# Three stack fills moved from ScalarE to GpSimd memsets, one semaphore per stack, and new orders on all engines

## The reference

```python
# 1: a convolution layer: bias, separable FIR upsampling by 2, leaky ReLU, FIR downsampling by 2
out = sep_upfirdn(input + bias, up_filter * 2, up=2)
out = leaky_relu(out, 0.2) * sqrt(2)
x = sep_upfirdn(out, down_filter, down=2)
# 2: attention on the 256 points of each image, 8 heads of 16 channels
x_norm = group_norm(x, g1, b1, 32 groups)
q, k, v = split(qkv_w @ x_norm + qkv_b)
attn = softmax(q k^T / sqrt(16)); a = out_w @ (attn v) + out_b
# 3: a gated MLP with 512 hidden channels, and a residual
a = group_norm(a, g2, b2, 32 groups)
h1, gate = split(mlp1_w @ a); return x + mlp2_w @ (silu(h1) * gate)
```

## Time and profile before

| | us |
|---|---|
| three executions | 145.64, 146.48, 148.33 (median 146.48) |
| the profiled execution | 146.12 |
| its span, first to last instruction | 144.3 |
| TensorE busy in it | 137.9 (96%) |
| ScalarE busy | 101.9 (71%) |
| VectorE busy | 94.0 (65%) |
| GpSimd busy | 69.4 (48%) |

### The profile page before, as it was taken

The page is one execution under the profiler, slowest core; times in us unless marked ns, Lnnn a source line. Parts: engine busy times, 40 slices in busy tenths (PEclk is TensorE's granted clock), DMA queues, the critical chain, the costliest instruction groups (busy, mean ns, idle before and its releaser), DMA issues.

```text
span 144.3 us, 3301 instructions
## 1 busy us (share of the span) xinstructions
PE 137.9 (96%) x1150; PEld 121.2 (84%) x1150; DVE 94.0 (65%) x194; ACT 101.9 (71%) x233; POOL 69.4 (48%) x121
## 2 busy tenths in 40 slices
PE   6999899999979999999999999999999999999992
PEld 5797789999969687779699699797897997999991
DVE  6959343477547878698799999573784714743251
ACT  6957878654639689398685996697886995966330
POOL 8300560840770595300870304894305898689930
PEclk9999999999999999999999999999999999999999
DMA  3899204564620160611604305210010010011012
GB/s 105 275 298 336 93 0 115 152 170 136 163 75 0 51 174 3 173 50 49 174 2 136 92 2 163 59 36 0 9 36 2 0 35 8 0 41 36 0 36 73
DMA packets 12368, 12.12 MB, mean 84 GB/s; under 512 B 1600, under 2 KB 11328, under 8 KB 12352
## 3 DMA queue, kind: packets, MB, share of 16 engines
q1 hardware_dynamic: 12208, 11.81, 27.6%
q10 hardware_dynamic: 144, 0.10, 0.2%
HBM read 4.50 MB, written 1.05 MB: 38 GB/s over the span
## 4 chain that ended last, share of the span: by engine, by line
PE 79%; SPq 8%; DMA 6%; DVE 4%; issue 1%; ACT 0%; POOL 0%; ACTq 0%; POOLq 0%
PE pm L852 11%; PE ps L878 11%; PE po L903 10%; SPq L287 5%; PE pf L765 4%; DMA win<-in_xh 4%; PE px L765 4%; PE pf L767 4%; PE pf L766 4%; PE pf L780 3%; PE px L766 3%; PE px L767 3%; SPq L314 3%; PE po L926 3%; PE ps L780 2%; PE px L834 2%
## 5 line engine op out<-in xcount | busy, mean ns | idle before, releaser
L1541 DVE TENSOR_REDUCE neg_max<-pm 128x2 f32<-128x512 f32 x64 | 42.0, 683 | 12.5 <-PE pm L852 12.2
L530 ACT ACTIVATE up_t<-ps 128x512 f32<-128x512 f32 x64 | 35.8, 596 | 7.3 <-PE ps L878 4.1
L878 PE MATMUL ps<-q_stack,k_stack 128*128 128x256 f32 x128 | 27.9, 301 | 0.9 <-DMA q_stack<-max_row 0.9
L852 PE MATMUL pm<-k_stack,q_stack 127*128 127x256 f32 x128 | 27.9, 305 | 0.2
L421 POOL TENSOR_TENSOR gated_lo<-win,gated_hi 128x512 fp32r<-128x512 f32 x14 | 18.1, 1299 | 16.4 <-ACT gated_hi L585 16.4
L852 PEld LDWEIGHTS pm<-k_stack,q_stack 127*128 127x128 f32 x128 | 19.6, 189 | 3.4 <-issue 1.5
L878 PEld LDWEIGHTS ps<-q_stack,k_stack 128*128 128x128 f32 x128 | 19.7, 189 | 2.4 <-DMA q_stack<-max_row 1.1
L903 PE MATMUL po<-up_t,v_aug 128*32 128x256 f32 x256 | 15.7, 382 | 0.0
L765 PE MATMUL pf<-xm_hi,w_hi 128*128 128x256 f32 x44 | 13.3, 303 | 0.2 <-issue 0.2
L585 ACT ACTIVATE gated_hi<-win 128x512 fp32r<-128x512 f32 x14 | 8.8, 631 | 5.3 <-DVE win L1590 3.4
L766 PE MATMUL pf<-xm_lo,w_hi 128*128 128x256 f32 x44 | 12.3, 280 | 0.0
(11 more groups left out here) (150 smaller groups left out, 334.4 us busy)
## 6 DMA issues: line engine op xcount, KB each, us to landing
q_stack<-qk_parts SPq DMA_DIRECT2D x24, 128.0 KB, 2.4
k_stack<-qk_parts SPq DMA_DIRECT2D x24, 128.0 KB, 2.4
win<-in_xw SPq DMA_DIRECT2D x12, 128.0 KB, 3.2
win<-in_xh SPq DMA_DIRECT2D x6, 256.0 KB, 5.0
out<-win SPq DMA_DIRECT2D x8, 128.0 KB, 1.7
win<-in_w SPq DMA_DIRECT2D x1, 512.0 KB, 3.7
w_s<-in_w SPq DMA_DIRECT2D x1, 256.0 KB, 3.7
wqk_s<-in_wqk SPq DMA_DIRECT2D x1, 128.0 KB, 4.2
```

The costliest lines, as they stand in the source:

```text
L530: act.activation(probs[:, h // HALF, h % HALF, :, :].rearrange("p c n -> p (c n)"), ps[:, h % 2, :], ACT.Exp, scale=D ** -0.5).then_inc(pr ...
L852: return pe.matmul(pm[:, h % 2, c * N:(c + 1) * N], stack_rows(q_stack, i, slice(0, TOP))[:, h, c * 128:(c + 1) * 128], stack_rows(k_stack ...
L878: return pe.matmul(ps[:, h % 2, c * N:(c + 1) * N], stack_rows(k_stack, i, slice(0, TOP + 1))[:, h, c * 128:(c + 1) * 128], stack_rows(q_s ...
L1541: dve.tensor_reduce(neg_max[:, i % 2, 2 * h:2 * h + 2], pm[:, h % 2, :].rearrange("p (c n) -> p c n", c=2), AX.X, ALU.max, negate=True).th ...
```

## The change

ScalarE keeps one fill (the q stack of slot 1). The k stack of slot 1 and both stacks of slot 2 are set by memsets on GpSimd, at the head of its list. Each slot has its own semaphore `stack_clear[r]`, which `stack(i)` waits for. The lists of all five engines stand in a new order.

```diff
-        stacks_clear = sem("stacks_clear")
-        first_clear = sem("first_clear")
+        stack_clear = [sem(f"stack_clear{r}") for r in range(SLOTS)]
...
-                if i == 0:
-                    sp.wait_ge(first_clear, 2)
-                elif i < SLOTS:
-                    sp.wait_ge(stacks_clear, 2 * i)
+                if i < SLOTS:
+                    sp.wait_ge(stack_clear[i], 2)
...
+            def clear_stack(r, j):
+                pool.memset((q_stack, k_stack)[j][r][:, :, :].rearrange("p h n -> p (h n)").bitcast(F32), j * 1.0).then_inc(stack_clear[r], 1)
...
+            clear_stack(1, 1)
+            clear_stack(2, 0)
             constants()
             clear_values()
+            clear_stack(2, 1)
             split_wqk()
...
-            def fill(r, j):
-
-                act.activation((q_stack, k_stack)[j][r][:, :, :].rearrange("p h n -> p (h n)"),
-                               rest[:, j:j + 1].to_broadcast([128, HEADS * N]), ACT.Copy).then_inc(stacks_clear, 1)
+            def fill():
+
+                act.activation(q_stack[1][:, :, :].rearrange("p h n -> p (h n)"),
+                               rest[:, 0:1].to_broadcast([128, HEADS * N]), ACT.Copy).then_inc(stack_clear[1], 1)
...
-            dve.memset(rest[:, 0:1], 0.0).then_inc(rest_ready, 1)
-            dve.memset(rest[:, 1:2], 1.0).then_inc(rest_ready, 1)
+            dve.memset(rest[:, :], 0.0).then_inc(rest_ready, 1)
```

More of the change, by code:

```diff
@@ L325, in store @@
                 sp.dma_start(out[b], result[:, b * N:(b + 1) * N]).then_inc(stored, 16)
-            stack(0)
-            stack(1)
+            for j in range(0, 3):
+                stack(j)
             load_w1()
-            stack(2)
             rows(0)
@@ L607, in _ @@
             read_y(1)
-            leaky(5)
-            fill(2, 0)
-            for j in range(6, 10):
+            for j in range(5, 8):
                 leaky(j)
-            fill(2, 1)
-            high_parts(0)
             read_y(2)
             read_y(3)
+            leaky(8)
+            high_parts(0)
+            leaky(9)
             leaky(10)
@@ L620, in _ @@
             read_y(4)
-            for j in range(12, 15):
-                leaky(j)
+            leaky(12)
+            leaky(13)
             read_early_v(1)
+            leaky(14)
+            high_parts(2)
             leaky(15)
-            high_parts(2)
             read_y(5)
@@ L632, in _ @@
             exponentials(0, 1)
-            high_parts(3)
+            read_early_v(2)
+            sum_biases()
             exponentials(0, 2)
             exponentials(0, 3)
-            sum_biases()
+            high_parts(3)
             exponentials(0, 4)
+            exponentials(0, 5)
             read_rows(1)
-            for j in range(5, 8):
-                exponentials(0, j)
+            exponentials(0, 6)
+            exponentials(0, 7)
             read_early_v(3)
+            read_sums(0)
@@ L675, in _ @@
[L675 removed]
+            square_attn(2)
             squash(0)
[L677 to L679 removed]
             high_parts(7)
+            split_high(0)
+            read_sums(3)
             squash(1)
[L682 removed]
             exponentials(4, 0)
             exponentials(4, 1)
[L685 removed]
+            spread_inverse(3)
+            for j in range(2, 5):
+                exponentials(4, j)
+            read_proj(3)
@@ L716, in _ @@
-            spread_inverse(5)
-            for j in range(3, 6):
-                exponentials(6, j)
-            read_proj(5)
+            squash(3)
+            read_sums(5)
+            exponentials(6, 0)
+            exponentials(6, 1)
+            split_high(3)
+            exponentials(6, 2)
+            spread_inverse(5)
+            exponentials(6, 3)
+            squash(4)
+            exponentials(6, 4)
+            read_proj(5)
+            exponentials(6, 5)
+            square_attn(5)
@@ L1001, in _ @@
             downsample(1)
-            upsample(5)
-            upsample(6)
+            for j in range(5, 8):
+                upsample(j)
             group_means(0)
-            for j in range(7, 10):
-                upsample(j)
             downsample(2)
+            downsample(3)
+            upsample(8)
             project_qk(0)
-            downsample(3)
+            group_means(1)
+            upsample(9)
             upsample(10)
             project_v(0)
-            group_means(1)
             upsample(11)
@@ L1019, in _ @@
             maxima(0, 1, 1)
-            upsample(12)
+            upsample(13)
             maxima(0, 2, 0)
-            upsample(13)
             maxima(0, 2, 1)
+            project_v(1)
             maxima(0, 3, 0)
@@ L1028, in _ @@
             maxima(0, 4, 1)
-            project_v(1)
+            project_qk(2)
             maxima(0, 5, 0)
@@ L1368, in _ @@
             weigh(6, 1, 1)
+            turn_maxima(7)
             up_project(6, 0, 0)
+            down_project(4, 0)
+            down_project(4, 1)
             up_project(6, 0, 1)
+            up_project(6, 1, 0)
+            turn_sums(6)
+            up_project(6, 1, 1)
+            turn_inverse(6)
             scores(7, 0, 0)
```

561 lines of the change are left out of this document (271 added, 290 removed).

## The result

The changed kernel is slower: 150.08 us median of four executions (149.46 to 150.46), against 147.1 us for the kernel before on the same chip. The ratio is 1.0233 with a 95% interval of 1.0128 to 1.0337. So it is slower, clear of noise; whether by more than 2% stays open. The forecast was 145.4 us in a range of 143.0 to 147.4, and a result over 149.4 had been given a chance of 0.04: it missed on the side, not just the size. The profiled execution took 150.46 us with a span of 148.6.

The account below looks back on a forecast made before the run. TensorE, busy 137.9 of 144.3 us, was taken as the bound, so only its waits counted. Terms 0.8 - 0.5 + 0.4 = 0.7 us off the profiled 146.12 gave 145.4 us, range 143.0 to 147.4.

Parts of the forecast that it names:

- The fills: Start, ScalarE to GpSimd: three memsets end by about 10.5 us, long before use, so moving them costs 0.
- 12 to 20 us: TensorE's hole before the group means at 15.06 takes `upsample(7)`: gain 0.87 us, bounds 0 and 1.3.
- First swap of SyncE: `load_w1` behind `stack(2)`: first scores at 41.1 instead of 42.35; TensorE stays 0.8 us ahead, bounds -0.4 and 1.5.
- The sum so far: Start through the first scores: TensorE 0.8 us ahead, the front and first SyncE swap counted as the same time.
- Second swap of SyncE: Image 2, `rows(2)` behind `stack(4)`: later scores mostly covered by 4.2 us of other work; -0.5 us, bounds -2.3 and 0.
- The rest of the orders: 45 to 140 us: a few shorter TensorE waits, only the direction derived; +0.4 us, bounds -2 and +3.
- The rows wait in SyncE's queue: Rival, images 2 and 4: rows behind stacks cost full price, 2.3 and 0.6 us, giving 148.2 us; chance 0.17.
- The hole moves: Rival: the gain at 14 us is given back at the next wait, giving 146.1 us; chance 0.25.
- the front: Start of the kernel: TensorE 0.8 us ahead after `upsample(7)` fills the hole and the first maxima come.

Follow-up runs that it names:

- e3: Kernel before with only the fills moved to GpSimd and a semaphore per slot, lists otherwise old: 146.52 us, ratio 1.001.
- e4: Kernel before with only SyncE's whole new list: 159.33 us, ratio 1.083.
- e7: e3 with `upsample(7)` moved ahead of `group_means(0)`: 146.92 us, ratio 1.004.
- e5: Changed kernel with `load_w1` right behind `rows(0)` instead of ahead of it: 148.99 us, ratio 1.020.
- e14: Changed kernel with the DMAs of the maxima rows issued from ScalarE's queue instead of SyncE's: 149.75 us, ratio 1.023.
- e1: Changed kernel with `rows(2)` ahead of `stack(4)` and `rows(4)` ahead of `stack(6)` again: 149.01 us, ratio 1.014.
- e10: e3 with the old orders up to about 56 us and the new orders on every engine behind it: 149.67 us, ratio 1.018.
- e15: e3 with the new orders on TensorE, ScalarE and VectorE only from 56 to 85 us, SyncE's list old: 150.00 us, ratio 1.024.
- e16: e3 with `weigh(1)` moved ahead of `maxima(3,1)` and `maxima(3,2)` on TensorE: 148.18 us, ratio 1.007.
- e2: Changed kernel with SyncE's whole old list: 149.41 us, ratio 1.018.
- e11: Changed kernel with the edits of e1 and e5 together: 147.74 us, ratio 1.008.
- e9: Changed kernel with its new orders up to about 56 us and the old orders on every engine behind it: 148.34 us, ratio 1.007.
- e12: e9 with `load_w1` behind `rows(0)`: 147.63 us, ratio 1.003.
- e17: e3 with `turn_sums(1)` and `turn_inverse(1)` ahead of the first scores of image 2: 152.16 us, ratio 1.029.

## Why the prediction was wrong

**The fills: right.** Nothing on GpSimd's side, done at 10.14 (forecast about 10.5); e3 1.001.

**12 to 20 us: right as told, worth less.** `upsample(7)` ran in the hole and the group means followed, but the start was late, as the first upsamples lay 0.43 instead of 0.22 us apart up to 5.87 us, so that the means came at 15.48 and not 15.06. The timeline, for the earlier trace rows:

```profile
13.76 1.89 PE L785 MATMUL pf<-win,up_w 128*128 128x256 f32 x8
...
15.48 0.28 PE L801 MATMUL po<-mv,gmat_s 128*128 128x4 f32 x2
```

What made the start late isn't the change's own doing, as far as can be told: the profiled executions of all the other kernels, e3 and e4 with their old orders on the compute engines included, begin with the wider spacing too, and change to 0.22 between 4.7 and 7.4 us. In each that has a record of the granted clock so early, that record begins, at 1.0, within 0.2 us of that moment (5.68 us here, 4.13 before, ahead of the first upsample). As 0.43 is twice 0.22, that looks like TensorE's 1.2 GHz level until then, but no row gives the clock of that stretch. By itself (e7) `upsample(7)` in the hole gave nothing.

**First swap of SyncE: half right.** Forecast first scores at 41.1, measured 41.78. I had taken a landing behind w1 of 41.0; w1 was issued at 37.40 and landed at 41.56, the rows right behind it. TensorE waits, for the earlier trace rows:

```profile
37.40 0.59 SPq L299 DMA_DIRECT2D win<-in_w  x1
38.03 0.57 SPq L317 DMA_DIRECT2D q_stack<-max_row  x1
...
41.78 0.62 PE L883 MATMUL ps<-q_stack,k_stack 128*128 128x256 f32 x3 [1.06 <-DMA q_stack<-max_row]
```

and the landing times of the row DMAs, for the earlier trace rows, and of w1, for the earlier trace rows:

```profile
DMA to landing us min/median/max: 1.8/2.0/3.7
```

```profile
DMA to landing us min/median/max: 4.2/4.2/4.2
```

The Trainium skill's rule ("DMA: Bandwidth & Descriptors", section "Queues, rings and completion order"), by which descriptors of one queue are consumed in ring order, was weighed against the 2.6 us of the earlier trace rows; here the trace agrees with it, as the rows landed 3.7 us after their issue and 0.18 us behind w1. With w1 behind them (e5) they took 2.4, and from ScalarE's queue (e14), issued at 37.24 while w1 was under way (36.91 to 41.70), they landed at 39.94, ahead of it. At 48 us TensorE was 0.5 ahead, not 0.8. The sum so far held.

**Second swap of SyncE: the mechanism was on paper, the size was wrong.** I took -0.5 from -2.3 to 0. Undoing it measured 0.9% (e1, not clear of noise), and it wasn't image 2, on which the working rested, but image 4, to which I gave 0.6 in the rival only. For image 2 I set 4.2 us of other work against the wait and argued that it hid most of 5.8. The work did hide the rows; but it was itself held by VectorE and ScalarE.

**The rest of the orders: this step failed.** "I can't derive more than the direction from that, and take +0.4" should have been a loss: the new orders behind 56 us cost 1.8%, 2.6 us (e10), of which the swap's share is some 0.9, so about -1.7 stands where +0.4 was taken; and e15, with none of SyncE's swaps, loses 2.4%. The direction came from lighter ScalarE and earlier images, neither of which bounded anything. What carried the answer was there to read: the sums and inverse ahead of the scores in the order pieces above, and `weigh(1)` ahead of `maxima(3,1)` in the lists of the two kernels. The earlier trace rows showed VectorE on the chain there, and the earlier trace rows that `weigh` takes 1.93 us: 1.93 us without a maximum for the engine that paces the stretch. That was to be had before the run, and e16 measured 1.0 us for it alone.

**What no term held.** The row DMA of image 1 that met an instruction load, about 1.5 us in the profiled execution. The trace of before had a hint of it that I read as "a DMA behind a large one": the 2.13 us for two issues at 36.21 coincides with such a load at 36.27.

**The rivals.** "The rows wait in SyncE's queue", 148.2, came nearest. It is shown for the old order (e4), and the traces show it for image 4 (83.68 in the changed kernel, 0.05 us behind the landing of its rows); but it isn't the cause of the whole: with SyncE's old list 1.8% are left (e2), with the rows put first and w1 behind them 0.8% (e11), and without any swap the other engines' new orders cost 2.4% (e15). "The hole moves" is what e7 did.

The account of the 2.3%, or 3.4 us, is then, in us: 0.5 gained by the front at 48 us; 1.3 lost at 48 to 52 by the late rows of image 1 (net 0.8, and e9 measured 0.7% for all ahead of 56, though its own rows of image 1 were in time, so that what it lost there is open); and about 2.6 lost behind 56 us (e10), of which the swap of image 4 is some 0.9 and `weigh(1)` ahead of the maxima 1.0. What is left, about 0.7 us, no run took apart. The account mixes steps of one profiled execution with ratios, and the pieces don't fit to better than some 0.5 us: each of these programs meets its instruction loads at other places. That the orders behind 56 us hold most of the loss is shown; the shares of the single places are argued from traces. No version beat the kernel before; e3, e7 and e12 are level with it.

## What to carry to other kernels

In lists of in-order engines, look for long work of the busiest engine (here 1.9 us of `weigh`) and ask which other engine has nothing queued while it runs: work for that engine belongs ahead of it. A small DMA on which the critical engine waits should stand ahead of large or many ones in its queue, but whether that matters depends on what else TensorE has to do, so SyncE's new list cost 8% in one order, and undoing its row swaps gave 0.9% in another. Here, an order made as a whole couldn't be judged or mended by its pieces: price a reorder by the waits at every place it touches, and give an unexplained remainder bounds on both sides of nothing.

## What was not expected of the hardware

**Instruction loads.** Nine loads of 16 KB on their own queue in each profiled execution, 0.9 to 1.9 us long. A row DMA of 8 KB issued 1.0 to 1.5 us ahead of one landed after 3.05 to 3.8 us instead of 1.8 (13 of 13), whether it left from SyncE's or ScalarE's queue, and two DMA issues on SyncE took 2.38 or 2.43 us instead of 1.2. In e11 and e12 an issue 0.3 us earlier or later made 1.5 us. That the load is the cause is read from where the slow ones fall; no run moved a load.

**The clock behind a long wait.** In e4 (SyncE's new list in the old kernel) the granted clock fell behind the wait of 4.69 us:

```profile
80.00:84.00 4.00, 0.06 (x1) 0.00 (x0) 0.44 (x1) 0.00 (x0) 0.00 (x0) 0.88 0.68 192
84.00:86.00 2.00, 1.24 (x5) 1.15 (x5) 0.41 (x1) 0.00 (x0) 0.00 (x0) 0.50 0.03 9
...
88.00:90.00 2.00, 2.00 (x12) 2.00 (x12) 0.79 (x2) 0.84 (x2) 0.00 (x0) 0.54 0.05 12
90.00:92.00 2.00, 2.00 (x37) 1.22 (x35) 1.71 (x4) 1.50 (x3) 0.64 (x1) 1.00 0.00 0
```

TensorE is idle from 80 to 84.7 us, and then runs at 0.50, its 1.2 GHz level, until near 90, with 5 to 12 matmuls in 2 us, against 37 right after. Five us of work at half the rate is some 2.5 us, an estimate from these rows: the wait of 4.69 us cost more than itself. e17 had the same behind two waits of 1.66 and 1.40 us close together. The changed kernel had neither: no window of it shows less than 1.0, with waits up to 1.24 us.
